# Eight neighbouring sets for the largest values, and logits contracted over 128 rows

## What is computed

```python
q = X @ W1.T @ W2.T              # 2048 x 64
k = X @ W3.T                     # 2048 x 64
logits = q @ k.T                 # contraction over 64
probs = softmax(logits)
# of each row keep the largest entries until their sum reaches 0.9
A = probs * mask
A = A / A.sum(-1)
Xf = R @ Xf                      # R: adj with its rows scaled
Xa = A @ Xa
Z = Z + Xf @ U1[n].T + Xa @ U2[n].T
```

## Time and profile before

| | us |
|---|---|
| the runs shown | 1213.11, 1197.78, 1226.84; median 1213.11 |
| the profiled execution | 1203.27, of which the span from first to last instruction is 1201.5 |
| busy in the span | PE 887.8 (74%), DVE 850.8 (71%), ACT 482.6 (40%), POOL 70.8 (6%) |
| mean granted TensorE clock | 0.807 of full |

### The profile page before, as it was taken

How to read it: one execution, slowest core, us unless ns; L and a number is a source line. 1 busy time by engine, 2 the same in 40 slices (tenths; PEclk the granted TensorE clock), 3 DMA queues, 4 the chain that set the end, 5 groups by cost and what they waited for, 6 DMA issues and landing times.

```text
span 1201.5 us, 11820 instructions
## 1 busy us (share of the span) xinstructions
PE 887.8 (74%) x3706; PEld 579.5 (48%) x3706; DVE 850.8 (71%) x2420; ACT 482.6 (40%) x848; POOL 70.8 (6%) x49
## 2 busy tenths in 40 slices
PE   5799878944887868079788458868590599997396
PEld 5744336623655658074255137547580464543142
DVE  5878579779969989921598799699799851133623
ACT  5784222265575485032222744844940220023111
POOL 0120010100000000000001000000030110002111
PEclk9899758855977988586588569879895799998598
DMA  9678014310022030000044000300350559300000
GB/s 348 267 286 335 9 70 145 113 40 2 1 70 80 1 115 35 0 1 1 0 140 138 3 1 1 106 35 1 106 182 0 207 188 376 140 0 1 0 10 26
DMA packets 21434, 107.56 MB, mean 90 GB/s; under 512 B 1888, under 2 KB 9584, under 8 KB 11120
## 3 DMA queue, kind: packets, MB, share of 16 engines
q1 hardware_dynamic: 19968, 106.12, 23.9%
q10 hardware_dynamic: 1392, 0.61, 0.2%
HBM read 86.79 MB, written 19.93 MB: 89 GB/s over the span
## 4 chain that ended last, share of the span: by engine, by line
issue 34%; PE 33%; DVE 16%; ACT 12%; POOL 2%; DVEq 1%; DMA 1%; POOLq 0%; ACTq 0%; SPq 0%
PE PS L661 11%; DVE AT L1236 7%; PE PS L722 7%; PE PS L897 5%; ACT BC L1082 4%; ACT AT L1082 4%; PE PS L464 3%; DVE mxv L1374 2%; PE PS L530 2%; DVE AT L1792 2%; ACT EA L1050 1%; PE PS L628 1%; PE PS L625 1%; ACT AT L1050 1%; DVEq L1477 1%
## 5 line engine op out<-in xcount | busy, mean ns | idle before, releaser
L661 PE MATMUL PS<-K,ST 64*128 64x512 f32 x240 | 170.5, 876 | 82.2 <-ACT EA L1050 61.7
L913 ACT ACTIVATE AT<-PS 128x512 f32<-128x512 f32 (+2 forms) x240 | 119.3, 560 | 202.8 <-PE PS L464 178.6
L464 PE MATMUL PS<-ident,AT 128*128 128x128 f32 x544 | 88.7, 300 | 104.6 <-issue 44.4
L661 PEld LDWEIGHTS PS<-K,ST 64*128 64x128 f32 x240 | 62.4, 270 | 166.7 <-issue 166.3
L1792 DVE MAX8 AT<-AT 128x8 f32<-128x256 f32 x256 | 138.3, 606 | 0.8
L464 PEld LDWEIGHTS PS<-ident,AT 128*128 128x128 f32 x544 | 71.6, 157 | 115.3 <-issue 50.6
L1236 DVE SCALAR_TENSOR_TENSOR AT<-EA,se 128x2048 uint8<-128x2048 f32 (+1 forms) x50 | 116.8, 2345 | 1.5 <-PE PS L464 0.7
L1374 DVE TENSOR_REDUCE mxv<-PS 128x1 f32<-128x2048 f32 x32 | 73.1, 2286 | 39.8 <-PE PS L661 39.8
L1236 DVE SCALAR_TENSOR_TENSOR AT<-AT 128x2048 uint8<-128x2048 f32 (+2 forms) x44 | 91.0, 2068 | 1.5 <-PE PS L464 0.6
L722 PE MATMUL PS<-hr,AT 128*128 128x128 f32 x512 | 72.2, 292 | 7.7 <-ACT AT L913 6.8
L722 PE MATMUL PS<-AT 128*128 128x128 f32 x512 | 73.2, 295 | 5.4 <-ACT AT L913 4.8
(11 more groups left out here) (261 smaller groups left out, 1383.0 us busy)
## 6 DMA issues: line engine op xcount, KB each, us to landing
AT<-keep_at SPq DMA_DIRECT2D x32, 1024.0 KB, 5.0
EA<-in_adj SPq DMA_DIRECT2D x24, 1024.0 KB, 6.3
keep_at<-AT SPq DMA_DIRECT2D x8, 2048.0 KB, 24.8
AT<-keep_at SPq DMA_DIRECT2D x7, 2048.0 KB, 12.8
AT<-in_adj SPq DMA_DIRECT2D x8, 1024.0 KB, 8.3
EA<-keep_degrees SPq DMA_DIRECT2D x1, 1024.0 KB, 6.4
keep_x<-K SPq DMA_DIRECT2D x4, 256.0 KB, 8.5
keep_z<-T SPq DMA_DIRECT2D x8, 128.0 KB, 3.4
```

The source lines that it names most:

```text
L464: return pe.transpose(dst, src, ident[0:p, 0:p])
L661: mm = pe.matmul(bank(half(gi, k) + n), ST[1][0:DA, k * P:(k + 1) * P], keys[:, n * BK:(n + 1) * BK], start=True, stop=True)
L913: return act.activation(dst, src, ACT.Copy)
```

## The change

1. Set s of the eight is now columns 256*s to 256*s+255, neighbours in memory, instead of every eighth column. The count and the size of the instructions stay.
2. The logits contract 128 rows instead of 64: the same K and ST[1], but all their partitions (`wide_keys`). So that the product stays what it was, partitions 64 to 127 of K and of ST[1] are set to zero by POOL, once, ahead of the first logits: K in four blocks of 64 x 512, each after its x1 was written out (x1_dma), and ST[1] after PE has turned the last block of the first layer's result that stood in it (ps_t). PE waits for zero_ok before the first logits and again before those of the fourth key block.
3. For that, POOL's loop over four powers is written out.

The diff, without the two hunks that only name the new semaphore zero_ok:

```diff
@@ -131,6 +131,7 @@
         XT = sb("XT", [P, N])
         XR = XT[:, :].rearrange("p (t c) -> p t c", c=P)
         keys = K[0:DA, :, :].rearrange("p t c -> p (t c)")
+        wide_keys = K[:, :, :].rearrange("p t c -> p (t c)")
         ST = [sb(f"ST{i}", [P, BK]) for i in range(2)]
         T = sb("T", [P, G, P])
         WT = sb("WT", [P, 9, P])
@@ -415,9 +416,27 @@
             power(Dn[:, :], rs[:, :], 0, NT, n + 1)
             power(ndr[:, :], nd[:, :], 0, NT, n + 2)
             n += 2
-            with pool.Fori(0, NB) as i:
-                power(sm[:, 3, :], sm[:, 2, :], 0, G, n + 1 + i)
+            def keys_zeroed(b, count):
+
+                pool.wait_ge(x1_dma[b], 16)
+                if count > 0:
+                    pool.wait_ge(zero_ok, count)
+                pool.memset(K[DA:P, b * G:(b + 1) * G, :], 0.0).then_inc(zero_ok, 1)
+
+            for b in range(NB - 1):
+                power(sm[:, 3, :], sm[:, 2, :], 0, G, n + 1 + b)
+            pool.wait_ge(pw_out, n + NB - 1)
+            for b in range(NB - 1):
+                keys_zeroed(b, b)
+            pool.wait_ge(ps_t, 1 + NB)
+            pool.wait_ge(zero_ok, NB - 1)
+            pool.memset(ST[1][DA:P, :], 0.0).then_inc(zero_ok, 1)
+            pool.wait_ge(zero_ok, NB)
+            power(sm[:, 3, :], sm[:, 2, :], 0, G, n + NB)
             n += NB
+            pool.wait_ge(pw_out, n)
+            keys_zeroed(NB - 1, NB)
+            pool.wait_ge(zero_ok, NB + 1)
             power(esc[:, :], cs[:, :], 1, NT, n + 1)
             n += 1
             for gi in range(STEPS * NB):
@@ -643,7 +662,7 @@
 
             def logit_part(k, n):
 
-                return pe.matmul(bank(4 * k + n), ST[1][0:DA, k * P:(k + 1) * P], keys[:, n * BK:(n + 1) * BK],
+                return pe.matmul(bank(4 * k + n), ST[1][:, k * P:(k + 1) * P], wide_keys[:, n * BK:(n + 1) * BK],
                                  start=True, stop=True)
 
             def logits(step, g, k):
@@ -658,8 +677,8 @@
                 if gi in BOTH and k == 1:
                     pe.wait_ge(mean_ok, gi + 1)
                 for n in range(4):
-                    mm = pe.matmul(bank(half(gi, k) + n), ST[1][0:DA, k * P:(k + 1) * P],
-                                   keys[:, n * BK:(n + 1) * BK],
+                    mm = pe.matmul(bank(half(gi, k) + n), ST[1][:, k * P:(k + 1) * P],
+                                   wide_keys[:, n * BK:(n + 1) * BK],
                                    start=True, stop=True)
                 mm.then_inc(logits_ok, 1)
 
@@ -745,6 +764,7 @@
             for step in range(STEPS):
                 if step == 0:
                     pe.wait_ge(q_out, 1)
+                    pe.wait_ge(zero_ok, NB)
                     for n in range(3):
                         pe.wait_ge(k_out, n + 1)
                         logit_part(0, n)
@@ -753,6 +773,7 @@
                     hr_turned(3)
                     keys_of(3)
                     pe.wait_ge(k_out, 4)
+                    pe.wait_ge(zero_ok, NB + 1)
                     logit_part(0, 3).then_inc(logits_ok, 1)
                     logit_part(1, 3)
                     means(0, 0)
@@ -1789,7 +1810,7 @@
                             next_max(k + 2)
                         if s == SETS // 2 and k == 2 and left > 0:
                             guess_gap(gi + 1)
-                        v.put(dve.max(tops[0][:, k, s * TOP:(s + 1) * TOP], cands[k][:, s:N:SETS]))
+                        v.put(dve.max(tops[0][:, k, s * TOP:(s + 1) * TOP], cands[k][:, s * N // SETS:(s + 1) * N // SETS]))
                     if k == 2 and left > 0:
                         guess_first(gi + 1)
                         dve.sem_inc(th_ok, 1)
```

More of the change, by code:

```diff
@@ L236, in gnn_kernel @@
             sure_steps ksum_ok mean_mm mean_ok lnz_ok gap_ok guess_steps guess_ok
-            cs_ok at_saved un_half un_st un_t un_row un_pr un_z th_ok sum_ok roots_ok fin_sq bias_ok h2_t h2_st hw_mm x2_ok"""
+            cs_ok at_saved un_half un_st un_t un_row un_pr un_z th_ok sum_ok roots_ok fin_sq bias_ok h2_t h2_st hw_mm x2_ok zero_ok"""
         (in_x, in_small, ident_ok, expo_ok, wt_t, wt_ok, nat_sum, nat_act, at_t, at_out, pw_in, pw_out,
@@ L245, in gnn_kernel @@
          ksum_ok, mean_mm, mean_ok, lnz_ok, gap_ok, guess_steps, guess_ok,
-         cs_ok, at_saved, un_half, un_st, un_t, un_row, un_pr, un_z, th_ok, sum_ok, roots_ok, fin_sq, bias_ok, h2_t, h2_st, hw_mm, x2_ok) = [sem(n) for n in names.split()]
+         cs_ok, at_saved, un_half, un_st, un_t, un_row, un_pr, un_z, th_ok, sum_ok, roots_ok, fin_sq, bias_ok, h2_t, h2_st, hw_mm, x2_ok, zero_ok) = [sem(n) for n in names.split()]
         slab_in = [sem(f"slab_in{i}") for i in range(2)]
```

## The result

The changed kernel takes 1152.3 us in the median of four runs (1151.6 to 1153.1), the kernel before 1212.9 on the same chip (1197.8 to 1226.8): a ratio of 0.954, 95% interval 0.945 to 0.963. Forecast were 1170, a range of 1148 to 1197, and faster with a chance of 0.80. The side and the range are right, the gain is larger than the forecast. The profiled execution took 1152.8 us, 50.5 less than the 1203.3 before, where my sum had 40.2.

A forecast was written before the change was run, and what follows sets the result against it. No engine was full; the order of time bound the kernel: cold PE logits at step starts, waits between engines, DVE alone in last groups. Terms 5.0 + 9.8 + 4.6 + 3.7 + 5.6 + 11.8 - 0.3 = 40.2 off 1210.2 gave 1170, range 1148 to 1197.

The forecast's parts named there:

- MAX8: DVE's MAX8 over 256 values: 606 to 413 ns with neighbours, counted as 184 ns each, 47 us over all 256.
- the bound of nothing: Lower bound for MAX8 on DVE: no saving, if it needed 2.05 ns an element whatever the step.
- the last groups: Groups 3 and 7: DVE alone is the path, all 32 MAX8 count, 5.9 us each, 11.8 together.
- Zeros count for the clock: Padded logits on PE raise its clock; the rival, chance 0.12, said zeros do not count, giving 1195 us.
- the start of step 1: First logits to next queries of step 1: padded passes turn warm, net 9.8 us saved.
- Start of step 0: First logits of step 0: 64-row passes lower the clock by 136.14, padding keeps it up, net 5.0 us saved.
- gi = 0: First group of step 0, after the start: cold tile 1.3, warm unit behind it 1.8, MAX8 1.5; net 4.6 us.
- gi = 4: First group of step 1, after the start: as in step 0 with a shorter cold unit, 3.7 us saved.
- Middle groups: Groups 1, 2, 5 and 6: 1.4 us saved each, 5.6 in all; remaining MAX8 savings end in DVE's wait for ACT.
- the two bounds by DVE's maxima: In groups 1, 2, 5, 6, exp of tiles 1 and 2 cannot precede their maxima, limiting the gain to 1.4 us.
- rival of looser chains: All 47 us of DVE's savings count and cold tiles give some 20, so 1143 us; chance 0.05.
- The branch `surely`: Rival, chance 0.04: eight values above the cut in one set trigger this branch, about 160 us more, to 1330.

The follow-up runs named there:

- e11_changed_again: The changed kernel itself, unchanged, run again beside the kernel before: 1152.1 us, ratio 0.950.
- e1_sets_only: The kernel before with only the neighbouring MAX8 sets; logits still contract 64 rows and nothing is zeroed: 1192.4 us, ratio 0.988.
- e4_wide_in_rest: The changed kernel with 64-row logits in groups 0 and 4 and the very first logits, 128 rows in the other six groups: 1170.4 us, ratio 0.970.
- e12_before_again: The kernel before itself, unchanged, profiled a second time: 1199.7 us in one execution.
- e7_stepped_in_middle: The changed kernel with sets of every eighth column again in groups 1, 2, 5 and 6 only: 1163.3 us, ratio 0.968.
- e2_rows_only: The changed kernel with only the sets undone: logits over 128 rows, sets still every eighth column: 1183.7 us, ratio 0.979.
- e9_both_maxima_earlier: The changed kernel with DVE's maxima of the next group's tiles 1 and 2 moved earlier in middle groups: 1147.6 us, ratio 0.947.

## Why the prediction was right, and where it was short

- **MAX8** was priced at 413 ns and takes 412, so the step does cost something and the bound of nothing is out. The sum then took 184 ns a piece where its own price gives 193. The 32 of gi = 3 take 6.2 us less (17.0 to 10.9), and the last groups, where DVE alone is the path, gave 6.8 and 6.1 for 5.9 each.
- **Zeros count for the clock.** That rival, at 0.12, is out: the clock is 0.91 at the start of step 1. The start alone is worth 10.5 us by the queries (32.31 to 21.82) for 9.8 foreseen; its 32 passes end after 17.17 us for about 18. Another execution of the same kernel, `e11_changed_again`, began them warm and took 15.64, and two other kernels with 128 rows took over 18.3, so that the figure was met so closely is in part luck.
- **Start of step 0, the step that was false.** I read the low clock at 136.14 as the effect of ten 64-row passes. `e1_sets_only`, `e4_wide_in_rest` and `e12_before_again` have the same passes and full clock there. In `e1_sets_only` it is low a little later, at 140.58 (2.07 us for two passes); in the other two it holds up to the wait ahead of the 16 passes. All ten traces with padded rows hold it that far too. So 64 rows do not always lose the clock here. That padding keeps it is suggested by two of four against none of ten, not shown. The difference makes 3.5 us in the table. The first queries come 5.9 us earlier (167.76 to 161.89) for 5.0, but of that up to 3.5 need not be the change's: `e4_wide_in_rest`, warm at 136, puts 3.1 on padding, which is the 5.0 without the 1.9 that I had given the four passes at 138.88.
- **gi = 0, mis-sized.** The sum had 4.6 for it. Of the 15.4 up to its masks, 5.9 are the start, 9.5 are left. The lone tile saved 2.7 and not 1.3: it took 4.47 us where I had estimated 5.9, so the clock rose early within it. The units behind it run warm, PE waits 1.87 us for ACT's copy before the product ahead of the queries in place of 3.24, and the clock is up behind it: L644, L647 and L659 take 1.04, 1.07 and 1.05 us in place of 1.94, 1.96 and 1.86. I had followed the warm clock for one unit and no further. ACT's guess comes 13.0 us sooner and its first sum 15.4 (234.92 for 250.29), the 5.9 of the start included. A part is luck: `e7_stepped_in_middle` has the same code in gi = 0, its lone tile took 5.81, near my estimate, and its masks come 99.5 us after the first queries for 96.4.
- **gi = 4** gave, with the start of step 1, 15.0 for 13.5.
- **Middle groups, mis-sized by the same neglect.** From first to third tile, the part that I worked out, the gain is 1.39 us in gi = 1 (28.31 to 26.92) and 1.79 in gi = 5, for 1.4: the two bounds by DVE's maxima were read well. What I left out is the clock behind the third tile. In gi = 5 the third tile to the queries takes 19.25 us (690.02 to 709.27) where it took 21.09 (730.63 to 751.72), since the clock no longer falls behind that tile (granted 0.85 from 740.4 to 751.7 before, 1.00 from 700.4 to 709.3 now). In gi = 1 it is the other way: 21.93 where it was 18.80. There the padded chain waits for DVE, the clock falls and the third tile takes 5.37 for 3.67; warm queries and a warm tile for the next group (3.70 at 323.49 for 7.17 at 338.76) give only part of that back. So 0.7 lost in one group and 2.4, 3.6 and 3.5 won in the three others: 8.8 for 5.6. A share of the rival of looser chains was true then, but not by DVE's 47 us counting in full.
- **The two edits are not a sum.** I added their terms, with 0.7 of the 1.4 a middle group for each. 14 us by the medians and 15 by the profiles come only when both are there, which `e1_sets_only` and `e2_rows_only` show.
- **Waits on DVE's side** came as foreseen in place and sign, not in size: gi = 0's wait for ACT's sums grew from 4.55 to 5.31 us only, because ACT came sooner too. In gi = 1, 2, 5 and 6 it went from 4.54 to 5.36, from 1.96 to 5.11, from 5.35 to 5.36 and from 3.77 to 5.34, where I had let 4.5 us a group of DVE's savings end in it. DVE in the changed kernel:

```profile
251.01 0.16 DVE L1257 SCALAR_TENSOR_TENSOR se<-below,AT 128x4 f32<-128x4 f32 x1 [5.31 <-ACT BC L1103]
```

- **The zeros** cost nothing: the first logits are at 130.33 for 130.06 before, no wait on POOL stands there, and a memset of 512 columns takes 519 ns.
- **The branch `surely`** was not taken; the masks with 32-bit output are 64 as before.
- **The rest** came out 1.5 longer in the changed kernel. It is 267.7 in one execution of it and 266.3 in another, so this is not the change either.
- **Median and profile.** The changed kernel's runs span 0.1%, those of before 2.4%. Before's median was 1212.9, 1210.2, 1202.5 and 1212.6 on the occasions measured, so part of the 60 us between the medians depends on which of these one meets; from fastest to fastest run it is 46 (1197.8 to 1151.6). The longer executions of before have the lower mean granted clock: 0.811 at 1200.4 us, but 0.798 to 0.804 in the seven of 1210 to 1217 beside it. None of these was profiled, so in which stretches the clock was lower beyond the 3.5 us at the start of step 0 stays open.

## What to carry to other kernels

Where two engines alternate over a buffer, each in turn the later one, speeding up one of them can bring little and even cost, as in gi = 2, 5 and 6 here: the one that is early waits, and behind such waits TensorE's clock sometimes fell. Look at both waits of the pair before an edit is priced, and when one side is made faster, move the other side's release (here the maximum) ahead of work that nobody waits for, at all places of the pair at once. When a stretch becomes warm, follow the clock through to the next long wait, not only to the next unit. Choose sets for MAX8 over float32 with a step of one or two; four cost as much as eight (602 and 606 ns for 412 and 414). Other DVE instructions were not measured at steps of two and four.

## What the hardware showed that was not expected

- Behind passes over 96 and 128 rows, a third or half of them zeros, TensorE's clock rises from 1.2 to 2.4 GHz. Behind 32 passes over 64 rows, begun at 1.2 GHz, it did not in 27.65 us, in four traces. When it rises varies between executions of the same passes over 128 rows: the first 16 at the start of step 1 took 7.13 to 10.02 us. The one trace of 96 rows has 10.18.
- MAX8 over 256 float32: 412, 414, 602 and 606 ns with steps of 1, 2, 4 and 8.
- The clock is not a function of the last wait alone: in gi = 1 of the changed kernel the tile after a wait of 3.08 us is warm (3.67) and the next, after 2.02 us, is not (5.37), while in gi = 5 it is, after 1.79. Behind a wait of 2.15 us in gi = 5 the clock held in the changed kernel and fell in `e9_both_maxima_earlier`. What decides between such close cases was not settled.
